# A two-layer cross-attention kernel on one core: the transposed softmax goes from SBUF to SBUF, and three steps named `acc` stand elsewhere in the order

## The chip, the core and the metric

The kernel runs on one NeuronCore of a Trainium2 chip. Its engines are TensorE (PE in the profile; its weight loads are PEld), VectorE (DVE), ScalarE (ACT), GpSimd (POOL) and SyncE (SP), each with an instruction stream of its own that is worked off in order and waits on semaphores. Matmuls write PSUM, and the other engines move data between PSUM and SBUF. DMA transfers are issued from an engine's queue, here SP's and ACT's. The metric is the device time of the whole program in microseconds. The median before is 1039.65 us of 3 runs, 1038.39 to 1040.42.

## The reference

For each of 8 batches, with x1 = x[b] and x2 = ctx[b], both 512 channels by 1024 positions:

```
q = Wq x1 + bq ; k = Wk x2 + bk ; v = Wv x2 + bv        (64, 64 and 512 rows)
x = v softmax(q^T k)^T + x1                             (softmax over k's positions)

theta = th_w x + th_b ; phi = phi_w x2 + phi_b ; g = g_w x2 + g_b   (256 rows each)
y = (theta^T phi / 1024) g^T  ->  w_w y + w_b, batch norm with stored statistics, + x
```

The second layer has no softmax. The kernel therefore multiplies phi and g first: phi g^T is taken from the 512 x 512 matrix x2 x2^T (the "gram") and from the row sums of x2.

## The kernel before

Matmuls keep the precision of fp32 by splitting each operand into a high part (a copy rounded to fp32r) and a low part (the rest), and by multiplying three pairs of parts. So almost each operand costs ScalarE a copy and VectorE or GpSimd a subtraction.

The order of the work is written out by hand. `FIRST` (batch 0) and `LATER` (batches 1 to 7) hold, for each of `pe`, `act`, `dve` and `pool`, a string of steps such as `S:3` or `v:0`, and `order()` turns it into the sequence that the engine runs. A plus sign marks work for the next batch. The steps that matter here:

- `S:t` (t = 0 to 7): scores of 128 queries against all keys. TensorE multiplies, VectorE takes the maximum, ScalarE the exponential, VectorE scales (`n:t`) and transposes 32 x 32 blocks (`tr:t`) into the tiles `tp0`, `tp1`, two t to a tile.
- `move(b, p)` on SP turns pair p of them into the full transpose: it writes both tiles to a DRAM tensor `turn` (2 transfers of 512 KB) and reads it back into `mv1` or `mv2` in another order (8 transfers of 128 KB).
- `T:t`: ScalarE (`do_T`, line 832) and VectorE (line 996) split `mv` into the operand `pt` of the product with v, which TensorE runs as `PV`. PV of half 0 waits for the low part of T:3, PV of half 1 for that of T:7.
- `x2T:m`: the split of the transposed context for the gram (`L`, `G` on TensorE).
- `k`, `q`, then `k2`, `q2`: sums and splits of k and q. S:0 waits for `klo` and `qlo`, the results of `k2` and `q2` on VectorE.
- `v:m`: v for 128 positions. The PSUM bank of TensorE's `v:2` in the later batches is the one that VectorE's `v:0` frees, that of `Y:0` in batch 0 the one that VectorE's `v:6` frees.
- `acc`: a bias row of 256 numbers from phi_w and the row sums of x2. In batch 0 GpSimd computes it in 17 instructions after a scaling of `br` (lines 1084 to 1095) and in the later batches VectorE does in 8 (line 913). ScalarE's `acc` (line 796) takes the high part and waits for the eighth sum; `accl` (line 918 on VectorE) or the end of GpSimd's `acc` gives the low part, and TensorE's `psi` (line 631) multiplies it.
- `s8` on GpSimd: four columns that VectorE's first `Y` needs.

Of the kernel before, what the change touches and what calls it, by code (L numbers as in the profile page):

```python
# [4 lines left out]
F = mybir.dt.float32  # L5
# [18 lines left out]
    k=2, q=2, S=8, GT=2, M=2, B=2, g=40, psi=1,  # L24
# [31 lines left out]
def use_g(b, r):  # L56
# [28 lines left out]
    pool=(  # L85
        "x2T:0 x2T:1 x2T:2 x2T:3 x2T:4 x2T:5 x2T:6 x2T:7 s8 acc Y:0 Y:1 Y:2 Y:3 PV:0,0 PV:0,1 PV:0,2 PV:0,3 PV:1,0 "
        "PV:1,1 PV:1,2 PV:1,3"
# [10 lines left out]
    act=(  # L98
# [6 lines left out]
    dve=(  # L105
# [26 lines left out]
def xattn_kernel(nc, x, ctx2, ctx2T, wkT, wqT, wvT, wpgT, thT, woT, brow, cols, out):  # L132
    with ExitStack() as stack:
        def sem(name):
            return stack.enter_context(nc.semaphore(name))
# [3 lines left out]
        def at(name, shape, dt, offset):  # L139
            return nc.alloc_sbuf_tensor_at(name, shape, dt, offset=offset)  # L140
# [69 lines left out]
        qlo = at("qlo", [128, 1024], R, o)  # L210
        mv2 = at("mv2", [128, 4, 2, 256], F, o); o += 4096
        P = at("P", [128, 1024], F, o)
# [13 lines left out]
        bm = at("bm", [128, 2, 2, 512], R, o)  # L226
        mv1 = at("mv1", [128, 4, 2, 256], F, o)
        x2T_f0 = at("x2T_f0", [128, 4, 512], F, o); o += 8192
# [6 lines left out]

        turn = nc.dram_tensor("turn", [4, 128, 4, 2, 256], F).ap()
        s_turn = [sem(f"s_turn{t}") for t in range(8)]
        sems = {n: sem("s_" + n) for n in PER}
# [54 lines left out]
        def mv(p):  # L293

            return mv2 if p == 3 else mv1
# [24 lines left out]
        def moved(i):  # L320

            j = i % 2 * 2
            return [mv(i // 2)[:, j:j + 2, t, :].rearrange("p j (u n) -> p u j n", u=8) for t in range(2)]

# [50 lines left out]
        def _(eng):  # L375
# [24 lines left out]
            def move(b, p):  # L400


                for t in range(2):
                    wait(eng, "tr", b, 2 * p + t)
                    eng.dma_start(turn[p, :, :, t, :], tp[p % 2][:, t, :].rearrange("p (i n) -> p i n", i=4))\
                        .then_inc(s_turn[2 * p + t], 16)
                for t in range(2):
                    eng.wait_ge(s_turn[2 * p + t], 16 * (b + 1))
                for k in range(2):
                    if p == 0:  # L410
                        wait(eng, "x2Tlo", b, 7)
                    elif p == 3:
                        wait(eng, "S", b, 7)
                    else:
                        wait(eng, "Tlo", b, 2 * p - 2 + k)
                    for i in range(4):
                        eng.dma_start(mv(p)[32 * i:32 * i + 32, 2 * k:2 * k + 2, :, :],
                                      turn[p, 64 * k:64 * k + 64, i, :, :].rearrange("(j a) t n -> a j t n", a=32))\
                            .then_inc(s_mv[2 * p + k], 16)

# [285 lines left out]
        def _(eng):  # L706
# [118 lines left out]
            def do_T(b, t):  # L825
                eng.wait_ge(s_mv[t], 64 * (b + 1))
                if t == 0:
                    wait(eng, "g", b, use_g(b, 3))
                if t == 4:
                    wait(eng, "M", b, 1)  # L830
                for k in range(2):
                    last = act(pt_half(t, HI)[k], moved(t)[k], ACT.Copy)  # L832
                done(last, "Thi")
# [36 lines left out]
        def _(eng):  # L870
# [87 lines left out]
            def do_tr(b, t):  # L958
                wait(eng, "norm", b, t)
                if t == 2:  # L960
                    wait(eng, "x2Tlo", b, 3 if b else 7)
                if t >= 4:
                    for i in range(2):
                        eng.wait_ge(s_mv[t // 2 * 2 - 4 + i], 64 * (b + 1))
                done(eng.transpose(tp[t // 2 % 2][:, t % 2, :], P[:, :]), "tr")  # L965
# [19 lines left out]
            def do_Y(b, c):  # L985
                wait(eng, "g", b, G_Y + c)
                if c == 0:
                    eng.wait_ge(s_br8, 1)
                    wait(eng, "s8", b)
                done(stt(out=yf[:, c, :], in0=br[:, :], scalar=scol8[:, c:c + 1], in1=bank_of(G_Y + c)[:, 0:256],  # L990
                         op0=ALU.mult, op1=ALU.add), "gf")
# [171 lines left out]
```

## Time and profile before

| | us |
|---|---|
| median of 3 runs | 1039.65 |
| the profiled execution | 1039.65 |
| its span | 1037.8 |
| TensorE busy | 1028.6 (99%) |
| VectorE busy | 685.1 (66%) |
| ScalarE busy | 494.9 (48%) |
| GpSimd busy | 296.4 (29%) |

The granted TensorE clock is 1.00 over the span. The chain that ended last is TensorE for 89%, VectorE for 4%, GpSimd and DMA for 2% each. The costliest group is the product with v (line 661): 353.8 us in 1536 matmuls. The DMA queues moved 155.46 MB, and the write to `turn` and the reads from it land 3.2 and 2.9 us after their issue (medians). A row of the timeline gives the start of a run of like instructions, how long it took, their count, and in brackets how long the engine had stood idle before it and who released it. Times are counted from the start of the span.

### The profile page before, as it was taken

The numbers are of one execution on the slowest core, as the hardware profiler recorded it, in microseconds if no ns is written. First come the engines' busy times: TensorE is split into PE (matmuls) and PEld (weight loads), VectorE is DVE, ScalarE is ACT, GpSimd is POOL, SyncE is SP. The second block draws the span as 40 slices with busy tenths as digits, with TensorE's granted clock in tenths as the row PEclk, the third lists the DMA queues.
The fourth block names the chain that finished last, engine by engine and source line by source line (L and its number), as shares of the span: only waits on it lengthen the run. The fifth ranks groups of instructions, "written<-read, shape, count | busy, mean of one in ns | idle before, by whom it ended". The sixth has DMA issues, their size and how long they took to land.

```text
span 1037.8 us, 13692 instructions
## 1 busy us (share of the span) xinstructions
PE 1028.6 (99%) x5055; PEld 850.6 (82%) x5055; DVE 685.1 (66%) x970; ACT 494.9 (48%) x835; POOL 296.4 (29%) x253
## 2 busy tenths in 40 slices
PE   9999999999999999999999999999999999999998
PEld 7778888888888887888888888888887888878887
DVE  6994497834888258882588825887268862688625
ACT  7653564425554264542744427454275532655321
POOL 1652370122701236012360123502144022540220
PEclk9999999999999999999999999999999999999999
DMA  7747153561545514455244552455434464335602
GB/s 255 217 142 234 65 200 123 163 222 54 170 129 189 190 63 161 139 186 183 72 153 152 178 178 87 137 163 181 165 103 136 150 201 142 122 123 163 193 31 81
DMA packets 94226, 155.46 MB, mean 150 GB/s; under 512 B 10064, under 2 KB 43728, under 8 KB 94160
## 3 DMA queue, kind: packets, MB, share of 16 engines
q1 hardware_dynamic: 84944, 137.80, 40.6%
q10 hardware_dynamic: 9216, 16.78, 4.8%
q8 instruction: 41, 0.67, 0.3%
q14 instruction: 25, 0.20, 0.1%
HBM read 104.22 MB, written 50.33 MB: 149 GB/s over the span
## 4 chain that ended last, share of the span: by engine, by line
PE 89%; DVE 4%; POOL 2%; DMA 2%; ACT 1%; issue 1%; SPq 0%; ACTq 0%; DVEq 0%
PE pG L661 33%; PE pG L567 14%; PE pG L672 8%; PE pG L575 6%; PE pG L606 4%; PE pG L582 4%; PE pT L694 3%; PE pG L694 3%; PE pS L618 2%; PE pM L649 2%; PE pT L514 2%; PE pT L618 2%; PE pM L640 2%; PE pS L503 2%; POOL x1s L1067 1%; DMA x2T_f<-in_ctx2T_dram 1%
## 5 line engine op out<-in xcount | busy, mean ns | idle before, releaser
L661 PE MATMUL pG<-pt,vT 128*128 128x512 f32 x1536 | 353.8, 389 | 0.0
L661 PEld LDWEIGHTS pG<-pt,vT 128*128 128x128 f32 x1536 | 286.9, 188 | 58.6
L1103 POOL TENSOR_TENSOR xms<-xr,xms 128x512 fp32r<-128x512 f32 x64 | 87.4, 1372 | 327.6 <-ACT xms L854 327.6
L567 PE MATMUL pG<-wv,x2s 128*128 128x512 f32 x720 | 169.3, 392 | 0.3
L567 PEld LDWEIGHTS pG<-wv,x2s 128*128 128x128 f32 x720 | 133.9, 188 | 31.7 <-issue 2.5
L1019 DVE SCALAR_TENSOR_TENSOR xr<-pG,cl,xr 128x512 f32<-128x512 f32 x64 | 47.9, 749 | 167.8 <-PE pG L661 167.8
L854 ACT ACTIVATE xms<-xr 128x512 fp32r<-128x512 f32 x64 | 40.4, 631 | 174.9 <-DVE xr L1019 174.9
L996 DVE TENSOR_TENSOR pt<-mv,pt 128x512 fp32r<-128x512 f32 x128 | 83.3, 693 | 56.3 <-ACT pt L832 56.1
L1099 POOL TENSOR_TENSOR ys<-yf,ys 128x256 fp32r<-128x256 f32 x32 | 29.6, 926 | 284.0 <-ACT ys L823 284.0
L832 ACT ACTIVATE pt<-mv 128x512 fp32r<-128x512 f32 x128 | 73.3, 622 | 57.9 <-DMA mv<-turn 42.0
L1074 POOL TENSOR_TENSOR x2Ts<-x2T_f,x2Ts 128x512 fp32r<-128x512 f32 x64 | 86.2, 1374 | 37.3 <-ACT x2Ts L792 37.3
L672 PE MATMUL pG<-xms,wth 128*128 128x512 f32 x384 | 88.3, 389 | 0.0
L672 PEld LDWEIGHTS pG<-xms,wth 128*128 128x128 f32 x384 | 72.1, 188 | 15.0
L1067 POOL TENSOR_TENSOR x1s<-st,x1s 128x512 fp32r<-128x512 f32 x56 | 71.2, 1307 | 45.8 <-ACT x1s L744 45.8
L965 DVE STREAM_TRANSPOSE tp<-P 128x1024 f32<-128x1024 f32 x64 | 79.5, 1241 | 1.3
L779 ACT ACTIVATE vT<-pG 128x512 fp32r<-128x512 f32 x62 | 36.9, 598 | 73.4 <-PE pG L567 73.4
L575 PE MATMUL pG<-x2Ts 128*128 128x512 f32 x256 | 63.0, 397 | 0.2 <-POOL x2Ts L1074 0.2
L575 PEld LDWEIGHTS pG<-x2Ts 128*128 128x128 f32 x256 | 46.8, 188 | 15.5 <-issue 5.8
L792 ACT ACTIVATE x2Ts<-x2T_f 128x512 fp32r<-128x512 f32 x64 | 37.2, 623 | 42.4 <-DMA x2T_f<-in_ctx2T_dram 42.4
L785 ACT ACTIVATE P<-pT,nmax 128x1024 f32<-128x1024 f32 x32 | 35.7, 1115 | 38.9 <-DVE tp L965 36.6
L606 PEld LDWEIGHTS pG<-wpg,gram 128*128 128x128 f32 x384 | 47.5, 191 | 5.4 <-issue 4.8
L606 PE MATMUL pG<-wpg,gram 128*128 128x256 f32 x384 | 49.6, 285 | 1.7 <-DVE vT L946 1.7
(145 smaller groups left out, 1486.6 us busy)
## 6 DMA issues: line engine op xcount, KB each, us to landing
turn<-tp SPq DMA_DIRECT2D x64, 512.0 KB, 3.2
mv<-turn SPq DMA_DIRECT2D x256, 128.0 KB, 2.9
x2T_f<-in_ctx2T_dram SPq DMA_DIRECT2D x32, 512.0 KB, 4.8
xr<-in_x_dram ACTq DMA_DIRECT2D x64, 256.0 KB, 5.2
st<-in_ctx_dram SPq DMA_DIRECT2D x31, 512.0 KB, 6.4
st<-in_x_dram SPq DMA_DIRECT2D x29, 512.0 KB, 4.2
out_dram<-oh SPq DMA_DIRECT2D x32, 256.0 KB, 2.0
out_dram<-xr SPq DMA_DIRECT2D x31, 256.0 KB, 8.0
```

The costliest lines, as they stand in the source:

```text
L567: last = mm(bank, x2s[:, l, c, 128 * m:128 * m + 128], wv[:, r, c, :], start=(c == 0 and n == 0), stop=(c == 3 and n == 2))
L575: last = mm(bank, x2Ts[:, HI, m, 128 * r:128 * r + 128], x2Ts[:, LO, m, :], start=(m == 0), stop=(m == 7))
L606: last = mm(bank[:, 0:256], gram[:, l, d, 128 * c:128 * c + 128], wpg[:, r, d, 0:256], start=(d == 0 and n == 0), stop=(d == 3 and n == 2))
L661: last = mm(bank, vT[:, l, m, 128 * c:128 * c + 128], pt(h)[:, r, m, :], start=(m == 0 and n == 0), stop=(m == 7 and n == 2))
L672: last = mm(bank, wth[:, l, c, 128 * k:128 * k + 128], xms(h)[:, c, r, :], start=(c == 0 and n == 0), stop=(c == 3 and n == 2))
L694: last = mm(bank, bm[:, l, k, 128 * c:128 * c + 128], th[:, r, k, 512 * h:512 * h + 512], start=(k == 0 and n == 0), stop=(k == 1 and n == 2))
L832: last = act(pt_half(t, HI)[k], moved(t)[k], ACT.Copy)
L965: done(eng.transpose(tp[t // 2 % 2][:, t % 2, :], P[:, :]), "tr")
L996: last = tt(pt_half(t, LO)[k], moved(t)[k], pt_half(t, HI)[k].bitcast(F), ALU.subtract)
L1067: done(tt(x1s(b)[:, LO, c, cols], st1(b, c)[:, cols], x1s(b)[:, HI, c, cols].bitcast(F), ALU.subtract), "x1lo")
L1074: done(tt(x2Ts[:, LO, m, :], x2T_raw(b, m), x2Ts[:, HI, m, :].bitcast(F), ALU.subtract), "x2Tlo")
L1103: done(tt(xms(h)[:, c, LO, :], xr[c][:, :], xms(h)[:, c, HI, :].bitcast(F), ALU.subtract), "xlo")
```

## The change

Three things are changed.

1. `move` no longer goes through DRAM. For each pair it waits for the second transpose and then issues 16 transfers of 64 KB straight from `tp` to `mv`, four for each block j of 32 source partitions, all on SP's queue. The first eight count for T:2p, the last eight for T:2p+1. The tiles `mv1` and `mv2` hold the two t outermost, and the two places that read or await them are adapted.
2. ScalarE's `acc` stands earlier: in batch 0 right behind `GT:1`, ahead of `w:7` and `v:6` (it was behind `T:3`), in the later batches right behind `k`, ahead of `x2T:1` (it was behind `x2T:4`). VectorE's `accl` in the later batches stands ahead of `q` (it was behind it).
3. On GpSimd in batch 0, `acc` stands ahead of `s8`, and VectorE's first `Y` no longer waits for the scaled `br`, since `s8` now comes after it.

```diff
@@ -69,7 +69,7 @@
-        "S:3 T:0 G:1 G:2 T:1 G:3 GT:0 S:4 GT:1 w:7 v:6 v:7 T:2 S:5 T:3 acc Y:0 Y:1 Y:2 S:6 Y:3 psi S:7 w:8 xr:0 "
+        "S:3 T:0 G:1 G:2 T:1 G:3 GT:0 S:4 GT:1 acc w:7 v:6 v:7 T:2 S:5 T:3 Y:0 Y:1 Y:2 S:6 Y:3 psi S:7 w:8 xr:0 "
...
@@ -208,7 +208,7 @@
-        mv2 = at("mv2", [128, 4, 2, 256], F, o); o += 4096
+        mv2 = at("mv2", [128, 2, 4, 256], F, o); o += 4096
...
-        mv1 = at("mv1", [128, 4, 2, 256], F, o)
+        mv1 = at("mv1", [128, 2, 4, 256], F, o)
...
@@ -233,8 +233,6 @@
-        turn = nc.dram_tensor("turn", [4, 128, 4, 2, 256], F).ap()
-        s_turn = [sem(f"s_turn{t}") for t in range(8)]
...
@@ -320,7 +318,7 @@
-            return [mv(i // 2)[:, j:j + 2, t, :].rearrange("p j (u n) -> p u j n", u=8) for t in range(2)]
+            return [mv(i // 2)[:, t, j:j + 2, :].rearrange("p j (u n) -> p u j n", u=8) for t in range(2)]
...
@@ -400,23 +398,18 @@
             def move(b, p):
-                for t in range(2):
-                    wait(eng, "tr", b, 2 * p + t)
-                    eng.dma_start(turn[p, :, :, t, :], tp[p % 2][:, t, :].rearrange("p (i n) -> p i n", i=4))\
-                        .then_inc(s_turn[2 * p + t], 16)
-                for t in range(2):
-                    eng.wait_ge(s_turn[2 * p + t], 16 * (b + 1))
-                for k in range(2):
+                wait(eng, "tr", b, 2 * p + 1)
+                for j in range(4):
                     if p == 0:
                         wait(eng, "x2Tlo", b, 7)
                     elif p == 3:
                         wait(eng, "S", b, 7)
                     else:
-                        wait(eng, "Tlo", b, 2 * p - 2 + k)
+                        wait(eng, "Tlo", b, 2 * p - 2 + j // 2)
                     for i in range(4):
-                        eng.dma_start(mv(p)[32 * i:32 * i + 32, 2 * k:2 * k + 2, :, :],
-                                      turn[p, 64 * k:64 * k + 64, i, :, :].rearrange("(j a) t n -> a j t n", a=32))\
-                            .then_inc(s_mv[2 * p + k], 16)
+                        eng.dma_start(mv(p)[32 * i:32 * i + 32, :, j, :],
+                                      tp[p % 2][32 * j:32 * j + 32, :, 256 * i:256 * i + 256])\
+                            .then_inc(s_mv[2 * p + j // 2], 16)
...
@@ -823,7 +816,7 @@
-                eng.wait_ge(s_mv[t], 64 * (b + 1))
+                eng.wait_ge(s_mv[t], 128 * (b + 1))
...
@@ -985,7 +978,6 @@
                 if c == 0:
-                    eng.wait_ge(s_br8, 1)
                     wait(eng, "s8", b)
```

In the strings that aren't shown, GpSimd's `... x2T:7 s8 acc Y:0` has become `... x2T:7 acc s8 Y:0` in `FIRST`, ScalarE's `k x2T:1 x2T:2 x2T:3 x2T:4 acc x2T:5 q` has become `k acc x2T:1 x2T:2 x2T:3 x2T:4 x2T:5 q` in `LATER`, and VectorE's `acc k q accl v:0` has become `acc k accl q v:0`. The wait in `do_tr` counts to 128 like that in `do_T`.

ScalarE in batch 0, from the split of the gram's last block on. `accs_first` is the step `acc`, `wth` is `w:7`, `vT` is `v:6` and `v:7`, `pt` is `T:2`. Before:

```order
L819 ACTIVATE gram<-pM 128x2x128
L721 ACTIVATE wth<-wth_f 128x1024
L779 ACTIVATE vT<-pG 128x512 x2
L832 ACTIVATE pt_85<-mv_128 128x8x64 x2
L785 ACTIVATE P,rsum<-pT,nmax 128x1024
L832 ACTIVATE pt_85<-mv_128 128x8x64 x2
L796 ACTIVATE accs_first<-acc_first 128x256
L823 ACTIVATE ys<-yf 128x256 x3
```

Now:

```order
L812 ACTIVATE gram<-pM 128x2x128
L789 ACTIVATE accs_first<-acc_first 128x256
L714 ACTIVATE wth<-wth_f 128x1024
L772 ACTIVATE vT<-pG 128x512 x2
L825 ACTIVATE pt_85<-mv_128 128x8x64 x2
L778 ACTIVATE P,rsum<-pT,nmax 128x1024
L825 ACTIVATE pt_85<-mv_128 128x8x64 x2
L816 ACTIVATE ys<-yf 128x256 x3
```

`accs_first` has gone up past one split of weights, two of v, two of the turned softmax and an exponential.

ScalarE in batch 1, from the first piece of the transposed context on (`x2Ts`); `accs` is `acc`, and `qhi` is `q2`. Before:

```order
L792 ACTIVATE x2Ts<-x2T_f_126 128x512
L751 ACTIVATE k_101<-pS 64x1024
L792 ACTIVATE x2Ts<-x2T_f_126 128x512 x3
L792 ACTIVATE x2Ts<-x2T_f_129 128x512
L796 ACTIVATE accs<-acc 128x256
L792 ACTIVATE x2Ts<-x2T_f_129 128x512
L758 ACTIVATE q_105<-pT 64x1024
L779 ACTIVATE vT<-pG 128x512
L792 ACTIVATE x2Ts<-x2T_f_129 128x512 x2
L772 ACTIVATE qhi<-pT 128x1024
```

Now:

```order
L785 ACTIVATE x2Ts<-x2T_f_126 128x512
L744 ACTIVATE k_101<-pS 64x1024
L789 ACTIVATE accs<-acc 128x256
L785 ACTIVATE x2Ts<-x2T_f_126 128x512 x3
L785 ACTIVATE x2Ts<-x2T_f_129 128x512 x2
L751 ACTIVATE q_105<-pT 64x1024
L772 ACTIVATE vT<-pG 128x512
L785 ACTIVATE x2Ts<-x2T_f_129 128x512 x2
L765 ACTIVATE qhi<-pT 128x1024
```

`accs` has gone up past four pieces of the transposed context, which now stand between it and `q`.

VectorE in batch 1: the eight sums of `acc`, then `k` (`pM`), `q` (`pT`) and `accl` (`accs`). Before:

```order
L913 SCALAR_TENSOR_TENSOR acc<-wpg,scol,br 128x256
L913 SCALAR_TENSOR_TENSOR acc<-wpg,scol,acc 128x256 x7
L927 SCALAR_TENSOR_TENSOR pM<-pS,cl,k_101 64x256 x4
L933 SCALAR_TENSOR_TENSOR pT<-pT,cl,q_105 64x1024 x2
L918 TENSOR_TENSOR accs<-acc,accs 128x256
L946 TENSOR_TENSOR vT<-pG,vT 128x512
L942 TENSOR_TENSOR qlo<-pT,qhi 128x1024
L946 TENSOR_TENSOR vT<-pG,vT 128x512
L938 TENSOR_TENSOR klo<-pM,khi 128x512
```

Now:

```order
L906 SCALAR_TENSOR_TENSOR acc<-wpg,scol,br 128x256
L906 SCALAR_TENSOR_TENSOR acc<-wpg,scol,acc 128x256 x7
L920 SCALAR_TENSOR_TENSOR pM<-pS,cl,k_101 64x256 x4
L911 TENSOR_TENSOR accs<-acc,accs 128x256
L926 SCALAR_TENSOR_TENSOR pT<-pT,cl,q_105 64x1024 x2
L939 TENSOR_TENSOR vT<-pG,vT 128x512
L935 TENSOR_TENSOR qlo<-pT,qhi 128x1024
L939 TENSOR_TENSOR vT<-pG,vT 128x512
L931 TENSOR_TENSOR klo<-pM,khi 128x512
```

`accs` has changed places with the two instructions of `q`.

## Rows read from the trace of the kernel before

**Rows 1.** the page, part 1: TensorE's busy time
```profile
PE 1028.6 (99%) x5055; PEld 850.6 (82%) x5055; DVE 685.1 (66%) x970; ACT 494.9 (48%) x835; POOL 296.4 (29%) x253
```

**Rows 2.** who TensorE waited for: us in total, times, longest
```profile
PE pM L631 <- DVE accs L918: 0.8, 1, 0.8
```

**Rows 3.** timeline of TensorE, batch 0: start us, us, instruction, idle before
```profile
60.95 1.31 PE L606 MATMUL pG<-wpg,gram 128*128 128x256 f32 x9 [1.66 <-DVE vT L946]
```

**Rows 4.** timeline of ScalarE, batch 0
```profile
57.82 1.06 ACT L721 ACTIVATE wth<-wth_f 128x1024 fp32r<-128x1024 f32 x1
58.85 1.08 ACT L779 ACTIVATE vT<-pG 128x512 fp32r<-128x512 f32 x2
...
65.88 0.40 ACT L796 ACTIVATE accs_first<-acc_first 128x256 fp32r<-128x256 f32 x1
```

**Rows 5.** timeline of GpSimd, batch 0
```profile
62.63 0.74 POOL L1093 TENSOR_TENSOR acc_first<-accp,acc_first 128x256 f32<-128x256 f32 x1
```

**Rows 6.** timeline of VectorE, batch 0
```profile
60.17 0.68 DVE L946 TENSOR_TENSOR vT<-pG,vT 128x512 fp32r<-128x512 f32 x1
```

**Rows 7.** timeline of ScalarE, batch 4
```profile
529.44 2.18 ACT L792 ACTIVATE x2Ts<-x2T_f 128x512 fp32r<-128x512 f32 x4
531.74 0.42 ACT L796 ACTIVATE accs<-acc 128x256 fp32r<-128x256 f32 x1
532.07 0.62 ACT L792 ACTIVATE x2Ts<-x2T_f 128x512 fp32r<-128x512 f32 x1
532.59 1.01 ACT L758 ACTIVATE q<-pT 64x1024 f32<-64x1024 f32 x1
```

**Rows 8.** timeline of VectorE, batch 4
```profile
526.07 5.64 DVE L913 SCALAR_TENSOR_TENSOR acc<-wpg,scol,acc 128x256 f32<-128x256 f32 x7
...
533.63 2.61 DVE L933 SCALAR_TENSOR_TENSOR pT<-pT,cl,q 64x1024 f32<-64x1024 f32 x2 [0.21 <-ACT q L758]
536.16 0.93 DVE L918 TENSOR_TENSOR accs<-acc,accs 128x256 fp32r<-128x256 f32 x1
537.02 0.67 DVE L946 TENSOR_TENSOR vT<-pG,vT 128x512 fp32r<-128x512 f32 x1
...
539.35 0.67 DVE L938 TENSOR_TENSOR klo<-pM,khi 128x512 fp32r<-128x512 f32 x1
```

**Rows 9.** timeline of TensorE, batch 4
```profile
537.38 0.40 PE L631 MATMUL pM<-accs,ones_r 128*128 128x256 f32 x2
537.74 3.01 PE L567 MATMUL pG<-wv,x2s 128*128 128x512 f32 x12
540.69 0.50 PE L618 MATMUL pS<-khi,qhi 64*128 64x512 f32 x2
```

**Rows 10.** chain that ended last, in order of time: start us, us, what
```profile
374.34 10.89 PE pG L672 x48
...
503.09 10.88 PE pG L672 x48
...
630.60 10.88 PE pG L672 x48
```

**Rows 11.** transfers of line 417: issue ns min/median/max, then landing us
```profile
L417 SPq DMA_DIRECT2D mv<-turn x256: 302/427/1880, 45.6 to 981.0; - x128
...
DMA to landing us min/median/max: 2.4/2.9/5.0
```

**Rows 12.** SyncE's waits: us in total, times, longest
```profile
SPq L260 <- DMA turn<-tp: 98.3, 32, 4.7
```

**Rows 13.** timeline of VectorE, batch 4, later
```profile
578.97 1.29 DVE L996 TENSOR_TENSOR pt<-mv,pt 128x512 fp32r<-128x512 f32 x2
```

**Rows 14.** timeline of TensorE, batch 4, later
```profile
581.25 2.00 PE L661 MATMUL pG<-pt,vT 128*128 128x512 f32 x8
```

**Rows 15.** timeline of TensorE at the launch
```profile
1.44 4.21 PE L701 MATMUL pT<-warm 128*128 128x512 f32 x9 [1.44 <-DVE warm L1056]
...
8.64 0.61 PE L531 MATMUL pG<-wv,x2s 128*128 128x512 f32 x2
```

More of the change, by code:

```diff
@@ L85 @@
     pool=(
-        "x2T:0 x2T:1 x2T:2 x2T:3 x2T:4 x2T:5 x2T:6 x2T:7 s8 acc Y:0 Y:1 Y:2 Y:3 PV:0,0 PV:0,1 PV:0,2 PV:0,3 PV:1,0 "
+        "x2T:0 x2T:1 x2T:2 x2T:3 x2T:4 x2T:5 x2T:6 x2T:7 acc s8 Y:0 Y:1 Y:2 Y:3 PV:0,0 PV:0,1 PV:0,2 PV:0,3 PV:1,0 "
         "PV:1,1 PV:1,2 PV:1,3"
@@ L963, in do_tr @@
                     for i in range(2):
-                        eng.wait_ge(s_mv[t // 2 * 2 - 4 + i], 64 * (b + 1))
+                        eng.wait_ge(s_mv[t // 2 * 2 - 4 + i], 128 * (b + 1))
                 done(eng.transpose(tp[t // 2 % 2][:, t % 2, :], P[:, :]), "tr")
```

4 rows, old and new, of tables (act, dve) are left out of this document.

## The prediction

> **What bounds the kernel now.** I read the busy times first. TensorE is busy for 1028.6 us, 99% of the span [rows 1], so a faster transfer or a shorter chain elsewhere can give back only what TensorE idles, and whatever makes TensorE wait is added in full. The waits of TensorE come next: the longest is 1.66 us, once, for VectorE's low part of v [rows 3], and 0.8 us once for the low part of the bias row (`accs`) [rows 2]. The chain in order of time shows the period: the products with theta's weights start at 374.34, 503.09 and 630.60 us, so one period is 128.75 and the next 127.51 us [rows 10]. The longer one holds the 0.8 us wait and is 1.24 us over; six of the seven batches behind batch 0 show the short period to within 0.25 us. All that the change could win is these 1.24 us, about 0.25 us in batch 1, and part of the 1.66. So the question is whether one of the moved steps now stands in an engine's way. A moved step that waits blocks everything queued behind it, and for that I read ScalarE's, VectorE's and GpSimd's timelines around each new place.
>
> **Part 1: `acc` on ScalarE in batch 0.** It waits for GpSimd's eighth sum, which starts at 62.63 and takes 0.74, so it is there at 63.37 us [rows 5]. In its new place ScalarE reaches it at 57.82, where the split `w:7` starts now [rows 4]. ScalarE then stands still for 5.6 us, and `w:7`, `v:6`, `v:7` and T:2 are queued behind. After the wait the step takes 0.33 us to the next start (like 531.74 to 532.07 in [rows 7]; it is the 0.40 us row in batch 0), `w:7` 1.03 us (57.82 to 58.85), and the first of two copies of v half of 1.08 us [rows 4]: 63.42 + 0.33 + 1.03 + 0.54 = 65.3 us, and with a tenth for the semaphore 65.4 us. VectorE's low part of `v:6` starts at 60.17 us now [rows 6], not held by ScalarE. It becomes 5.2 us later, and TensorE's `Y:0`, which waits for it and starts at 60.95 us [rows 3], goes to 66.15. VectorE works the following steps (a transpose, `v:7`, a maximum, `Y:0`) back to back in its order, so they move by the same 5.2 us and nothing catches up. GpSimd's sums start as before, since what they wait for has not moved. They could end a little earlier while VectorE idles, or ScalarE could be slower: bounds 4.7 and 5.5, value **+5.2 us**.
>
> The Trainium skill speaks to the lower bound: "GPSIMD Engine Reference", section "Specifications", says that GpSimd's SBUF interfaces are shared with VectorE and that VectorE instructions with two SBUF inputs contend with it. By that rule the last sums would gain from VectorE's idle time; by the row, 0.74 us for the last one, there is little left to gain.
>
> **Part 2: TensorE's clock in that gap.** TensorE now idles 1.66 us before `Y:0` [rows 3]; it will idle 6.9. Full speed follows the 1.66 us. The only longer rest in the trace is the launch: there nine matmuls of 512 columns start within 4.0 us (1.44 to 5.44, 444 ns each), about the 1.2 GHz level, and from 8.64 us on two such take 0.61 us in all, where 1.1 would be due at the launch's rate, so that is the 2.4 GHz level [rows 15]. The granted clock is given as 1.0 throughout, so I read the level from the spacing. If the 6.9 us act like the launch, the next 6.7 us (the launch's lasted from 1.44 to somewhat before 8.64) run at half rate. `Y`'s matmuls of 256 columns start 0.13 us apart (nine in 1.31 us, [rows 3]) and would take 0.22, so 30 of them cost 6.7 instead of 3.9 us, 2.7 us lost in round numbers, less some 0.2 that TensorE would wait for VectorE anyway. Bounds 0 (as after 1.66 us) and 2.5; since 6.9 is four times the longest rest after which full speed is seen, I take a drop, and **+2.0 us** for it.
>
> The Trainium skill, "TensorE: Matmul & The Clock Gate", section "What's actually happening", says that an idle engine falls back to the 1.2 GHz level and rises only after sustained activity. By that the gap does cost clock. No row before the change shows such a fall inside the run.
>
> **Part 3: `acc` on ScalarE in batches 1 to 7.** It waits for VectorE's eighth sum, the end of a run that starts at 526.07 and takes 5.64 [rows 8], and starts at 531.74 us both now and then. Four pieces of the transposed context fill that time now, 529.44 to 531.62 [rows 7]. With `acc` ahead of them ScalarE waits 2.3 us behind `k`, and the pieces come after: next start 532.07, then five pieces of 0.52 us (532.07 to 532.59) give 534.67 for `q`, against 532.59 now [rows 7]: 2.08 us later. VectorE's `q` waits for it already [rows 8] and goes from 533.63 to 535.71. `accl` is no longer behind it, which wins 0.86 us (536.16 to 537.02). So `v:0` starts at 537.02 + 2.08 - 0.86 = 538.24. TensorE's `v:2` needs the bank that `v:0` frees: 0.72 us later as now (537.02 to 537.74, [rows 8, 9]), 538.96, so **1.22 us** late. S:0 then follows 2.95 us behind (537.74 to 540.69, [rows 9]); `klo`, now at 539.35 with 1.3 us to spare, comes some 1.8 us later at about 541.8 and just makes it. Nothing takes this back: VectorE's sums of the next batch start behind TensorE's last product. In the long period this delay replaces the one it has, so 0 there; six batches pay: 6 x 1.22 = **+7.3 us**. Bounds 6 x 1.0 and 6 x 1.4.
>
> **Part 4: the direct move.** Per pair, behind its second transpose, now: 98.3/32 = 3.1 us of wait for the write [rows 12], 8 issues of 0.427 us, 2.9 us to landing [rows 11], 9.4 us for the last piece and 7.7 for the first half. Then: 16 issues, 6.8 us, plus 2.9, is 9.7 us, and 6.3 for the first half. The trace has no transfer of this kind; the landings of the 128 KB pieces are 2.4 to 5.0 us, and I take the median, since those are small pieces into the same tiles. TensorE has no wait for `pt` in any batch, so either sign is hidden: **0**. Its cover in the tightest place is 1.0 us (VectorE's two subtractions for T:3 end at 580.2, and the first product with v starts at 581.25, [rows 13, 14]). SP's loads of the next batch and its stores are behind the move and have all of the product with v as cover. `s8` behind `acc` on GpSimd is needed by VectorE's `Y:0`, behind TensorE's at 66.15 us in the new schedule; behind the sums (63.37) come ScalarE's copy of 0.40 us [rows 4], one more subtraction of about 0.74 and `s8` itself, so it is there by 65 us: 0. The removed wait is implied by it: 0. The new tile layout changes strides and no instruction: 0.
>
> **Sum.** The profiled execution took 1039.65 us, which is the median too (span 1037.8 and 1.85 around it). 1039.65 + 5.2 + 2.0 + 7.3 = 1054.15, predicted **1054 us**.
>
> **Rivals.**
> - *The clock stays up.* For it: full speed behind 1.66 us of rest. Against: 6.9 us is far longer. 1039.65 + 5.2 + 7.3 = 1052.2 us. Here the skill's clock rule stands against it.
> - *Only one of the two stalls reaches TensorE*, because the chain behind it has slack that I don't see in the rows, for instance if VectorE's `v:0` does not wait behind `q`. 1039.65 + 7.2 or + 7.3: 1047 us. Against: both chains are followed step by step to TensorE with no free time between.
> - *The transfers come late.* If landings of SBUF to SBUF are all like the longest of now, 5.0 us, T:3's operand comes 0.3 + 2.1 = 2.4 us later, 1.4 beyond the cover, in each of 8 batches: 1054 + 11 = 1065 us. Half of it gives 1059. Against: half the bytes pass and none goes to DRAM.
> - *Faster.* The bias sums are done before ScalarE comes to the wait, and the earlier `accl` removes TensorE's wait for `accs`: 1039.65 - 1.24 - 0.25 = 1038.2 us. It decides if VectorE's eighth sum ended by 529.44 us, the end of `k`; it ends 2.3 us later [rows 7, 8], and GpSimd's 5.6 us later than needed. So this needs sums that take 60% of their time.
>
> **How the numbers follow.** Forecast 0.50 (1052.8 to 1055.8 its own range), clock stays 0.20, one stall alone 0.12, late transfers 0.08, faster 0.05, and 0.05 for effects that cancel to no change. A measurement of this kernel tells about 0.2% from no change, 2.1 us. Slower is 0.50 + 0.20 + 0.12 + 0.08 = 0.90, same 0.05, faster 0.05. The range reaches down over the one-stall case to 1046.5 and up to 1057.5 for part of the late transfers and the bounds of the sums; left out are faster, same and most of the late transfers, under 0.2.
>
> **What would show it.** In the profile after: ScalarE idle for over 5 us ahead of `accs_first`, TensorE idle for 6 to 7 us ahead of its first `Y`, and matmul spacing behind it near double (part 2), or not. In each later batch ScalarE idle for 2.3 us behind `k`, `q` about 2.1 us later, TensorE idle for 1.3 us between `psi` and `v:2`, and periods of 128.7 us all alike. No wait of TensorE for `pt`. I am wrong if periods stay at 127.5, if TensorE's gap in batch 0 stays below 3 us, or if TensorE waits for the products' operand.

## The result and the profile after

The changed kernel takes 1046.67 us (median of 4 runs, 1046.25 to 1047.21); the kernel before takes 1039.29 (4 runs, 1038.39 to 1040.42). The ratio is 1.007, 95% interval 1.0053 to 1.0088: slower, as forecast, by about half of the forecast's 14.5 us. 1046.67 lies at the low end of the range given (1046.5 to 1057.5). The profiled execution took 1045.72 us, its span is 1043.8, so 6.0 us of the two spans are to be explained. The medians lie 7.4 us apart: this profiled execution is 0.5 us below the fastest timed one of its kernel, and the one profiled before (1039.65) lies above the median of its kernel. In the experiments below, one execution of e6 (4481 us) and one of the kernel before (2072 us) lie far off all others and are left out of the ratios. Lines of this kernel are 7 lower than before up to the wait that `do_Y` has lost, and 8 lower behind it.

The page after, part 1, beside [rows 1]: TensorE's busy time grows by only 0.5 us, VectorE's shrinks by 6.4.

```profile
PE 1029.1 (99%) x5055; PEld 852.4 (82%) x5055; DVE 678.7 (65%) x970; ACT 495.2 (47%) x835; POOL 293.4 (28%) x253
```

The chain in order of time, the product with theta's weights (start us, us, what), beside [rows 10]:

```profile
125.39 10.88 PE pG L665 x48
...
253.38 10.88 PE pG L665 x48
...
380.99 10.88 PE pG L665 x48
508.58 10.88 PE pG L665 x48
636.25 10.88 PE pG L665 x48
```

These starts give periods of 127.6 and 127.7 us, and 128.0 for the first, where 128.7 was forecast. In TensorE's timeline this product first starts at 118.90 before and 125.23 after. So batch 0 costs 6.33 us, and the seven periods behind it together take 893.73 us against 894.10, a gain of 0.37: 6.33 - 0.37 = 5.96, which is the 6.0 of the spans.

The 0.37 us can't be put down to the change. TensorE's wait for `accs`, which makes one period of the kernel before longer, comes and goes between executions: in the traces of e1, e2 and e11, which keep the old order in the later batches, it stands in another batch (seven periods of 894.56, 894.00 and 893.87 us), and in those of e4 and e13 in none (892.79 and 892.69). The four traces with the new order (this one, e3, e7 and e9) don't have it and take 893.73 to 894.10. So in the later batches the change costs 0.9 to 1.4 us against an execution without that wait, and about nothing against one with it.

**Batch 0 after.** ScalarE, beside [rows 4]:

```profile
63.42 0.42 ACT L789 ACTIVATE accs_first<-acc_first 128x256 fp32r<-128x256 f32 x1 [5.26 <-POOL acc_first L1085]
63.74 1.04 ACT L714 ACTIVATE wth<-wth_f 128x1024 fp32r<-128x1024 f32 x1
64.69 1.06 ACT L772 ACTIVATE vT<-pG 128x512 fp32r<-128x512 f32 x2
```

GpSimd, beside [rows 5], and VectorE, beside [rows 6]:

```profile
62.66 0.72 POOL L1085 TENSOR_TENSOR acc_first<-accp,acc_first 128x256 f32<-128x256 f32 x1
```

```profile
65.30 0.69 DVE L939 TENSOR_TENSOR vT<-pG,vT 128x512 fp32r<-128x512 f32 x1 [5.00 <-ACT vT L772]
```

TensorE, beside [rows 3]:

```profile
66.09 6.68 PE L599 MATMUL pG<-wpg,gram 128*128 128x256 f32 x36 [6.79 <-DVE vT L939]
72.71 0.50 PE L611 MATMUL pS<-khi,qhi 64*128 64x512 f32 x2
```

The stall goes from GpSimd's sum over ScalarE and VectorE to TensorE, which starts at 66.09 instead of 60.95 and then needs 6.68 us for 36 products. In stretches of the run (window us, its length, busy us of PE, PEld, DVE, ACT and POOL with counts, granted clock, DMA share, GB/s):

```profile
62.00:64.00 2.00, 0.00 (x0) 0.00 (x0) 0.00 (x0) 0.58 (x2) 1.39 (x3) 1.00 0.41 99
64.00:66.00 2.00, 0.00 (x0) 0.00 (x0) 0.70 (x2) 2.00 (x4) 0.86 (x2) 0.54 0.41 98
66.00:68.00 2.00, 1.91 (x9) 1.94 (x10) 2.00 (x3) 0.79 (x2) 0.00 (x0) 0.50 0.00 0
68.00:70.00 2.00, 2.00 (x11) 2.00 (x11) 1.82 (x3) 1.11 (x3) 0.00 (x0) 0.50 0.00 0
70.00:71.00 1.00, 1.00 (x7) 1.00 (x6) 0.96 (x4) 1.00 (x3) 0.00 (x0) 0.52 0.00 0
71.00:72.00 1.00, 1.00 (x10) 1.00 (x10) 0.97 (x2) 0.43 (x2) 0.48 (x1) 1.00 0.00 0
```

While TensorE idles the granted clock goes from 1.00 (the 2.4 GHz level) to 0.50 (1.2 GHz), and it is back at 1.00 some 5 us after the matmuls have begun: 9 to 11 of them in 2 us, then 10 in 1 us.

**Batch 4 after**, VectorE, beside [rows 8]; the times are later by 5.5 us throughout, so lengths and distances are to be compared:

```profile
531.56 4.58 DVE L906 SCALAR_TENSOR_TENSOR acc<-wpg,scol,acc 128x256 f32<-128x256 f32 x7
...
537.75 1.07 DVE L911 TENSOR_TENSOR accs<-acc,accs 128x256 fp32r<-128x256 f32 x1
540.14 2.61 DVE L926 SCALAR_TENSOR_TENSOR pT<-pT,cl,q 64x1024 f32<-64x1024 f32 x2 [1.32 <-ACT q L751]
542.66 0.67 DVE L939 TENSOR_TENSOR vT<-pG,vT 128x512 fp32r<-128x512 f32 x1
```

ScalarE, beside [rows 7]:

```profile
536.17 0.42 ACT L789 ACTIVATE accs<-acc 128x256 fp32r<-128x256 f32 x1 [1.14 <-DVE acc L906]
536.49 2.70 ACT L785 ACTIVATE x2Ts<-x2T_f 128x512 fp32r<-128x512 f32 x5
539.10 1.01 ACT L751 ACTIVATE q<-pT 64x1024 f32<-64x1024 f32 x1
```

TensorE, beside [rows 9]:

```profile
542.87 0.40 PE L624 MATMUL pM<-accs,ones_r 128*128 128x256 f32 x2
543.39 3.01 PE L560 MATMUL pG<-wv,x2s 128*128 128x512 f32 x12
546.34 0.50 PE L611 MATMUL pS<-khi,qhi 64*128 64x512 f32 x2
```

The seven sums take 4.58 us where they took 5.64, ScalarE waits 1.14 us where 2.3 were forecast, and TensorE goes from `psi` to S:0 in 3.47 us instead of 3.31. GpSimd shows why. Before:

```profile
526.40 1.31 POOL L1074 TENSOR_TENSOR x2Ts<-x2T_f,x2Ts 128x512 fp32r<-128x512 f32 x1 [1.70 <-ACT x2Ts L792]
530.13 9.36 POOL L1074 TENSOR_TENSOR x2Ts<-x2T_f,x2Ts 128x512 fp32r<-128x512 f32 x7 [2.43 <-ACT x2Ts L792]
```

After:

```profile
531.96 1.29 POOL L1066 TENSOR_TENSOR x2Ts<-x2T_f,x2Ts 128x512 fp32r<-128x512 f32 x1 [1.78 <-ACT x2Ts L785]
537.18 4.04 POOL L1066 TENSOR_TENSOR x2Ts<-x2T_f,x2Ts 128x512 fp32r<-128x512 f32 x3 [3.93 <-ACT x2Ts L785]
```

GpSimd's subtractions for the transposed context follow ScalarE's copies. Before, 1.31 us of them and the 1.58 us from 530.13 to 531.71 run beside VectorE's sums (2.9 us in all); after, with the copies held back behind `acc`, only 1.29 us do.

Single sums show what that does. A sum that GpSimd doesn't disturb takes 0.48 us. This one of the kernel before begins while GpSimd's first subtraction runs, and ends 0.28 us behind it (527.99 against 527.71). One of k's sums, which reads one of its two inputs from PSUM (`pS`), begins while another subtraction runs and keeps its length:

```profile
526.59 1.40 DVE L913 SCALAR_TENSOR_TENSOR acc<-wpg,scol,acc 128x256 f32<-128x256 f32 x1
...
531.39 1.48 POOL L1074 TENSOR_TENSOR x2Ts<-x2T_f,x2Ts 128x512 fp32r<-128x512 f32 x1
532.03 0.47 DVE L927 SCALAR_TENSOR_TENSOR pM<-pS,cl,k 64x256 f32<-64x256 f32 x1
```

Two of the seven sums are held in this way in each later batch before (1.40 to 1.60 us each), and one after (1.40 to 1.45 us).

**The transfers after**, beside [rows 11]: issue ns min/median/max and landing us min/median/max.

```profile
L410 SPq DMA_DIRECT2D mv<-tp x512: 585/596/1854, 42.5 to 988.9; - x171
...
DMA to landing us min/median/max: 2.0/2.0/5.6
```

An issue takes 0.596 us, not 0.427, and lands in 2.0 us, not 2.9. The bytes moved fall from 155.46 to 121.94 MB. TensorE doesn't wait for `pt` in this kernel.

### The profile page after: what moved, and what is told of

Same layout as the page of the kernel before. It is cut to its first block, busy times and chain, and to the rows that moved or that the text cites. A ratio compares the mean times of both kernels' runs of the same rounds, so it can differ in the third digit from the quotient of the medians.

```text
span 1043.8 us, 13884 instructions
## 1 busy us (share of the span) xinstructions
PE 1029.1 (99%) x5055; PEld 852.4 (82%) x5055; DVE 678.7 (65%) x970; ACT 495.2 (47%) x835; POOL 293.4 (28%) x253
## 2 busy tenths in 40 slices
DMA packets 80916, 121.94 MB, mean 117 GB/s; under 512 B 13136, under 2 KB 46800, under 8 KB 80848
## 4 chain that ended last, share of the span: by engine, by line
PE 86%; DVE 7%; ACT 3%; POOL 2%; issue 1%; DMA 0%; SPq 0%; ACTq 0%; DVEq 0%; POOLq 0%
PE pG L654 33%; PE pG L560 11%; PE pG L665 8%; PE pG L568 5%; PE pG L599 5%; PE pT L687 4%; PE pG L687 4%; PE pG L575 4%; DVE acc L906 3%; PE pS L611 2%; PE pM L633 2%; PE pM L642 2%; DVE pT L926 2%; PE pT L611 2%; ACT x2Ts L785 1%
## 5 line engine op out<-in xcount | busy, mean ns | idle before, releaser
L1066 POOL TENSOR_TENSOR x2Ts<-x2T_f,x2Ts 128x512 fp32r<-128x512 f32 x64 | 83.7, 1335 | 49.0 <-ACT x2Ts L785 49.0
L599 PEld LDWEIGHTS pG<-wpg,gram 128*128 128x128 f32 x384 | 49.6, 199 | 10.2 <-issue 9.7
```

What stands on the lines that cost most here:

```text
L599: last = mm(bank[:, 0:256], gram[:, l, d, 128 * c:128 * c + 128], wpg[:, r, d, 0:256], start=(d == 0 and n == 0), stop=(d == 3 and n == 2))
L1066: done(tt(x2Ts[:, LO, m, :], x2T_raw(b, m), x2Ts[:, HI, m, :].bitcast(F), ALU.subtract), "x2Tlo")
```

## The experiments

Each is told against the kernel before, run in turn on the same chip (medians 1038.6, 1039.2 and 1039.4 us in the three sets of runs). In a diff `-` is the kernel named first.

**e1: the direct move alone.** All parts of the change in `mv1`, `mv2`, `moved`, `move` and the counts of the waits; no step `acc` or `s8` moves.

> The kernel before with the direct move alone; all orders as before. My theory: TensorE never waits for the turned softmax, so the time is that of before, 1039.3 us, within 1 us either way, and the period stays near 127.5 us with one of 128.7. VectorE's eight sums (acc) in the later batches keep their 5.6 us for seven. Rival (DMA traffic): it was the traffic through DRAM that slowed VectorE's sums, so here they take about 4.6 us for seven, and the wait for accs in batch 3 goes: 1038 us.

1041.1 us (11 runs), ratio 1.0021 (1.0012 to 1.003): not free, against my theory. The sums take their 5.6 us as before, so the rival falls too. TensorE waits for the following (us in total, times, longest):

```profile
PE pM L624 <- POOL accs_first L1088: 1.2, 1, 1.2
...
PE pG L654 <- DVE pt L989: 0.8, 1, 0.8
```

Both stand in batch 0, and ScalarE's copies of the moved blocks show their origin:

```profile
54.65 1.15 ACT L825 ACTIVATE pt<-mv 128x512 fp32r<-128x512 f32 x2 [2.12 <-DMA mv<-tp]
...
60.67 1.16 ACT L825 ACTIVATE pt<-mv 128x512 fp32r<-128x512 f32 x2 [0.90 <-DMA mv<-tp]
...
65.79 1.16 ACT L825 ACTIVATE pt<-mv 128x512 fp32r<-128x512 f32 x2 [1.20 <-DMA mv<-tp]
```

The third starts at 64.84 before. It delays ScalarE's `acc` (65.88, [rows 4], to 66.85 us), and TensorE's `psi` waits for that. From `Y:0` to theta's product it is 59.72 us (60.60 to 120.32), before 57.95 (60.95 to 118.90): 1.77 us lost. Two of the seven periods behind it take 127.8 us instead of 127.5.

**e11: the same move in half as many transfers.** The kernel of e1, with

```
-  for i in range(4):
-      eng.dma_start(mv(p)[32 * i:32 * i + 32, :, j, :], tp[p % 2][32 * j:32 * j + 32, :, 256 * i:256 * i + 256])
+  for i in range(2):
+      eng.dma_start(mv(p)[64 * i:64 * i + 64, :, j, :], tp[p % 2][64 * (j % 2):64 * (j % 2) + 64, :, 256 * i:256 * i + 256])
```

> The kernel before with the direct move alone, as in the first of these runs, but each pair goes in 8 transfers of 128 KB instead of 16 of 64 KB; the same bytes move, and every block of the softmax's rows lands in another place than the reference wants. Theory A, the number of issues: each issue holds SyncE's queue for 0.60 us, so 8 of them take 4.8 us per pair instead of 9.5, the waits of the copies of pt in batch 0 (2.1, 0.9 and 1.2 us in the first run) go, the first product with theta's weights starts at 118.9 us +-0.4 as in the kernel before, and the time is 1039.0 +-0.8. Rival B, the transfer between two places of SBUF is itself slow (or an issue costs by its bytes, so 1.2 us each): the waits and the 1.4 us of batch 0 stay, time 1040.5 to 1041.5.

1039.78 us (11 runs), ratio 1.0004 (0.9995 to 1.0013). The issues:

```profile
L410 SPq DMA_DIRECT2D mv<-tp x256: 590/608/2036, 43.7 to 978.3; - x128
```

An issue costs 0.608 us with twice the bytes, so between 64 and 128 KB the price goes by the transfer and not by the byte. (The kernel leaves out the order in which the blocks have to land, so its result isn't the reference's; bytes and waits are those of the direct move.) The three copies of `pt` have no wait on the transfers, and from `Y:0` to theta's product it is 57.95 us again (62.23 to 120.18). Theory A holds; rival B falls. The absolute start that I had given for that product (118.9) is missed by 1.3 us, because this execution was already 1.3 us late before its first such transfer (the first product with `wq` on `x1s_first` starts at 24.95 us, before at 23.68), which the change can't reach.

**e2: ScalarE's `acc` in batch 0 alone.** In `FIRST`, `act`:

```
-  GT:1 w:7 v:6 v:7 T:2 S:5 T:3 acc Y:0
+  GT:1 acc w:7 v:6 v:7 T:2 S:5 T:3 Y:0
```

> The kernel before with ScalarE's acc of batch 0 ahead of w:7 and nothing else. My theory: this one word makes the whole loss: TensorE idles about 6.8 us ahead of its first Y (5.1 more than before), the granted clock falls to 0.50 behind it, and the time is 1045.5 to 1047 us. Rival (the loss is spread over the parts): the time rises by 4 us or less.

1045.58 us (5 runs), ratio 1.0065 (1.0052 to 1.0077). One line of the order makes nearly all of the loss. TensorE:

```profile
65.58 6.59 PE L606 MATMUL pG<-wpg,gram 128*128 128x256 f32 x36 [6.78 <-DVE vT L946]
```

with a granted clock of 0.50 from 64 to 70 us.

**e4: GpSimd's `acc` ahead of `s8` in batch 0 alone.** In `FIRST`, `pool`: `s8 acc` becomes `acc s8`.

> The kernel before with GpSimd's acc ahead of s8 in batch 0 and nothing else. I had costed this at nothing, with ScalarE's earlier acc as its cover. Without the cover: s8 waits for the low part, which waits for ScalarE's acc behind T:3 (65.9 us); s8 is there at 67.4 us and VectorE's first Y moves from 63.6 to 67.4, so TensorE waits about 3.5 us ahead of Y:2: 1043 us, or 1044 to 1045 if the clock falls in that gap. Rival (GpSimd's order has slack): 1039.3 us.

1043.6 us (4 runs), ratio 1.0047 (1.0033 to 1.0061). Alone, this edit costs what the prediction had at nothing: GpSimd's `acc` waits for ScalarE's, which is still at its old place, and `s8` with VectorE's `Y:0` waits behind it (67.49 us instead of 63.63). TensorE:

```profile
60.90 4.60 PE L606 MATMUL pG<-wpg,gram 128*128 128x256 f32 x24 [1.67 <-DVE vT L946]
68.07 2.61 PE L606 MATMUL pG<-wpg,gram 128*128 128x256 f32 x12 [2.58 <-issue]
```

In the change it is hidden, since ScalarE's `acc` is early there: `s8` ends at 64.95 us. It also shows the clock fall behind a rest of 1.67 us (24 products take 4.60 us; granted 0.50 from 62 to 65 us, and again from 69 to 71 us, behind the 2.58), where the same rest of 1.66 us before [rows 3] was followed by the full rate.

**e9: the change without its edits to batch 0's order.** `FIRST` as before, all else as after.

> The changed kernel with batch 0 in the order of before (ScalarE's acc behind T:3, GpSimd's s8 ahead of acc, the wait for the scaled br back). My theory: all of the loss was in batch 0, so 1038.8 us, within 0.6 of before. Rival (the later batches cost too): 1041 us or more.

1041.23 us (9 runs), ratio 1.0023 (1.0013 to 1.0033). 5.4 of the 7.4 us of the change are gone with one table. The rest is that of e1: TensorE waits 1.09 us for `accs_first` and 0.9 for `pt` in batch 0. I had expected 1038.8, still holding the move to be free. The rival has the time, but not the place: the seven later periods take 893.89 us, no more than before.

**e7: TensorE kept busy in the gap.** The changed kernel, and ahead of `Y:0` in batch 0 24 products whose result nobody reads:

```
+  if b == 0 and c == 0:
+      wait(eng, "exp", 0, 4)
+      for _ in range(24):
+          mm(pS[:, 0, :], wv[:, 0, 0, 0:128], wv[:, 0, 0, :], start=True, stop=True)
```

> The changed kernel with 24 matmuls of 512 columns that nothing reads, on TensorE between S:5 and Y:0 of batch 0, into a score bank that is free then. They fill 5.4 of the 6.8 us. Theory (the rest costs clock): the granted clock stays at 1.0, the first 36 matmuls of Y take 4.9 us instead of 6.7, and the time is 1.2 to 1.8 us under the changed kernel, 1045 us. Rival (the slow stretch has another cause, such as the order of the other engines): no gain, 1046.7 us.

```profile
59.09 5.73 PE L596 MATMUL pS<-wv 128*128 128x512 f32 x24
66.17 4.91 PE L603 MATMUL pG<-wpg,gram 128*128 128x256 f32 x36 [1.35 <-issue]
71.01 0.50 PE L615 MATMUL pS<-khi,qhi 64*128 64x512 f32 x2
```

The clock stays at 1.00, the 36 products take 4.91 us, and S:6 starts 1.70 us earlier than after (72.71): that is the clock's part, measured. But the time is 1048.42 us (4 runs), ratio 1.009 (1.0077 to 1.0104), beside 1046.67 and 1.007 (1.0053 to 1.0088) for the change. My expectation of 1045 is missed; the two intervals overlap, so it is not shown that the filler makes the kernel slower. In the trace the first product with theta's weights starts 3.1 us later than after (128.33 against 125.23), because TensorE comes to the second half of the product with v sooner than its operands do:

```profile
104.88 7.30 PE L658 MATMUL pG<-pt,vT 128*128 128x512 f32 x24 [2.39 <-DVE pt L992]
```

ScalarE's copy for T:7 waits 4.85 us for its transfer there; SyncE issues this batch's 64 transfers until 99.7 us. The clock falls again behind it (0.52 in 106 to 108 us). So the issues of part 4 have no cover left in batch 0 once the gap is filled.

**e3: `acc` and `accl` in batches 1 to 7 alone.** In `LATER`: ScalarE `k acc x2T:1`, VectorE `k accl q`, as in the change; the move through DRAM stays.

> The kernel before with the two words moved in the later batches (ScalarE's acc right behind k, VectorE's accl ahead of q), softmax still turned through DRAM. My theory now: ScalarE's copies and so GpSimd's subtractions no longer run beside VectorE's sums, which take 4.6 us for seven instead of 5.6; v:2 of TensorE starts only 0.1 to 0.2 us later than before, the periods are 127.6 us and all alike, and the time is 1039 us, within 0.6. Rival (DMA traffic of the turn made the sums slow): the sums take 5.6 us, v:2 is 1.2 us late in each batch, and the time is 1046 us, as I had predicted for this part.

1040.24 us (11 runs), ratio 1.0012 (1.0003 to 1.002). VectorE:

```profile
526.09 4.53 DVE L913 SCALAR_TENSOR_TENSOR acc<-wpg,scol,acc 128x256 f32<-128x256 f32 x7
```

The sums are short with the transfers of before, so it isn't the DMA's lighter load that shortens them. The periods are 127.6 to 127.7 us but for batch 1's 128.2. The time is above the 1039 +-0.6 that I expected, and far below the rival's 1046.

**e6: GpSimd held back, nothing else.** The kernel before, with every step `acc` at its old place; in GpSimd's `x2T`:

```
+  if b and m:
+      wait(eng, "acc", b, 7)
```

> The kernel before with one more wait: in batches 1 to 7 GpSimd's subtractions of the transposed context from the second on wait for VectorE's eighth sum. ScalarE's copies and the DMA traffic stay beside the sums. Theory A (GpSimd slows the sums): seven sums take 4.6 us instead of 5.6, ScalarE's acc and q come up to 1 us earlier, the wait for accs in batch 3 is gone, and the time is 1038 us. Theories B (ScalarE's copies) and C (DMA traffic): the sums stay at 5.6 us and the time at 1039.3 us or above it.

VectorE, then GpSimd:

```profile
524.95 4.52 DVE L913 SCALAR_TENSOR_TENSOR acc<-wpg,scol,acc 128x256 f32<-128x256 f32 x7
```

```profile
529.64 9.24 POOL L1076 TENSOR_TENSOR x2Ts<-x2T_f,x2Ts 128x512 fp32r<-128x512 f32 x7 [3.06 <-DVE acc L913]
```

Some of ScalarE's copies run beside the sums here as before (from 528.33 us on), so it isn't ScalarE either: it is GpSimd. One sum in each batch is still held, by the first subtraction, which has no wait. Periods are 127.28 to 127.30 us but for batch 1's 128.32, and the time is 1037.34 us (11 runs), ratio 0.9982 (0.9973 to 0.9991): less than both kernels, for one wait.

**e5: GpSimd beside all of the sums.** The changed kernel, with GpSimd's first subtraction of batches 1 to 7 made four times, one after the other (same result). 

> The changed kernel with GpSimd's first subtraction of the transposed context made four times over in batches 1 to 7 (same operands and result), so that GpSimd works beside VectorE's sums again while ScalarE stands still. Theory A (GpSimd beside VectorE slows the sums): seven sums take 5.3 us or more instead of 4.6, v:2 is late by about 1 us in each batch, and the time is 1046.7 + 7 x 0.7 to 1.0 = 1051.5 to 1053.7 us. Theory B (ScalarE's copies beside them slow the sums) and theory C (DMA traffic): the sums stay at 4.6 us and the time at 1046.7 us.

VectorE, then GpSimd:

```profile
411.80 7.32 DVE L907 SCALAR_TENSOR_TENSOR acc<-wpg,scol,acc 128x256 f32<-128x256 f32 x7
```

```profile
412.22 4.15 POOL L1069 TENSOR_TENSOR x2Ts<-x2T_f,x2Ts 128x512 fp32r<-128x512 f32 x3 [1.77 <-ACT x2Ts L786]
416.44 1.36 POOL L1073 TENSOR_TENSOR x2Ts<-x2T_f,x2Ts 128x512 fp32r<-128x512 f32 x1
```

1071.96 us (4 runs), ratio 1.0326 (1.0306 to 1.0346): right in kind, and far above what I expected. The sums grow by 2.74 us (four of the seven are held in each batch, each to 0.28 us behind the end of a subtraction) and the shorter periods by 2.7 (127.6 to 130.3). Three of the seven periods are 132, because the granted clock falls behind TensorE's waits of 3.29, 2.86 and 2.80 us; behind the other four, of 2.79 to 2.81 us, it stays at 1.00. I had reckoned with a longer wait only, on fewer slowed sums and at full clock.

**e13: another order in batch 0.** The kernel before; ScalarE's `w:7` behind T:2, VectorE's low part of `v:6` ahead of `n:4`.

> The kernel before with the order of batch 0 alone changed: ScalarE splits w:7 behind T:2, VectorE takes the low part of v:6 ahead of n:4. Theory: TensorE's 1.66 us wait ahead of its first product of Y is VectorE's low part of v:6, so it shrinks to under 0.7 and the time falls by 1.0 +-0.4 against the kernel before. Rival: the next wait takes its place, time within 0.3 us of the kernel before.

1039.44 us (11 runs), ratio 1.0003 (0.9994 to 1.0012). The 1.66 us wait splits into two of 1.02 and 1.04, the second ahead of the 13th product of `Y`. My theory is missed and the rival holds.

**e12: both together.** e6's wait, e13's order, and `accl` ahead of `q`.

> The kernel before with three changes of order: GpSimd's second to eighth subtraction for the transposed context waits for VectorE's eighth sum (batches 1 to 7); VectorE's low part of the bias row ahead of q's (batches 1 to 7); in batch 0 ScalarE splits w:7 behind T:2 and VectorE takes the low part of v:6 ahead of n:4. The move through DRAM stays. Theory: the shorter periods of 127.29 us of the run with GpSimd's wait stay, and in batch 0 the 1.66 us wait ahead of Y:0 shrinks to under 0.7: 1037.3 - 1.1 = 1036.2 +-0.6. Rival: the wait ahead of Y:0 is only put off to T:2 or w:7 behind it (TensorE waits for the split weight), and the time is 1037.3 +-0.4; no gain over the run with GpSimd's wait.

1037.18 us (11 runs), ratio 0.9982 (0.9973 to 0.9991): no gain over e6 that could be told, as the rival had it. e6 and e12 lie 1.9 and 2.2 us below the kernel before in their own sets, and over 9 us below the changed one.

## Why the prediction was right in sign and twice too large

The profiled execution was forecast at 1054.15 us and took 1045.72, 8.4 less. By its parts:

- **Part 1, right.** +5.2 forecast, +5.14 measured (66.09 against 60.95). Each step of the path came within 0.1 us, and e2 shows it alone.
- **Part 2, right in kind.** +2.0 forecast. The 36 products take 6.68 instead of 4.91 us, 1.77; e7 gives 1.70. Of the 6.92 us that the two make behind S:6, 0.46 are taken back ahead of `mts`, where TensorE waited 0.30 us before and doesn't now, and 0.13 in the product with `mts`, which takes 2.88 us instead of 3.01. Parts 1 and 2: 7.2 forecast, 6.33 measured. The launch's row was a fair model of the fall; the stay at the low level was 5 us where I had read up to 6.7 off it. The Trainium skill's rule on the idle clock ("TensorE: Matmul & The Clock Gate", section "What's actually happening") is borne out by the 0.50 rows for this gap; shorter rests went either way (e4, e5).
- **Part 3, the step that failed.** The term was six batches x 1.22 = +7.3; the seven periods together gave -0.37. The failed sentence is that ScalarE's `acc`, which waits for VectorE's eighth sum, "starts at 531.74 us both now and then". It took the length of the sums, 5.64 us, as fixed. They are long because GpSimd works beside them, and the same edit that makes ScalarE wait holds GpSimd's subtractions back: 4.58 us, 1.06 less. Put into the forecast's own chain, 1.22 - 1.06 = 0.16 per batch, and TensorE's way from `psi` to S:0 did grow by 3.47 - 3.31 = 0.16. Against it stands the wait for `accs` that one period before has (128.75 us) and none after; as said above, executions of the old order have it or not, so the two nearly cancel in these two traces by chance. The prediction's own sign of being wrong, periods that stay near 127.5 us, came in. The rest of that chain held: five copies behind `acc`, `q` late, `accl` won.
- **Part 4, wrong but covered.** Issues were costed at 0.427 us from transfers of another kind, and take 0.596: 16 of them 9.5 us per pair, not 6.8. Landing was 0.9 us shorter. Alone this costs 1.77 us in batch 0 (e1), where the pairs follow closer; I had looked for the tightest place in batch 4 only. In the change TensorE's gap of 6.79 us hides it, and in the later batches TensorE doesn't wait for it. `s8`'s zero is right in the change and wrong alone (e4).

The rival "only one of the two stalls reaches TensorE" gave 1047 us and has the time nearly to the point, by another mechanism than its own: the chain had no slack, its first link got shorter. That the time is met so closely is luck. The rival "faster" came nearer in kind, as it asked for shorter sums; it needed 60% of their time, and they took 81%. The forecast looked at the wrong side of the matter too: I had weighed what the sums in batch 0 gain when VectorE idles (0.74 to 0.72 us, nothing), and not what VectorE's sums gain when GpSimd does.

How far the mechanism goes can be counted in the traces. In all thirteen, a sum of `acc` in the later batches that begins while one of GpSimd's subtractions of 128x512 runs is held until 0.28 us behind its end, 115 of 115 times; it takes 1.39 to 1.51 us instead of 0.48 (up to 1.60 where the two begin together). With none held the seven would take 3.6 us (7 x 0.52 from start to start). One held gives 4.52 to 4.68 us (after, e3, e6), two 5.46 to 5.64 (before) and four 7.25 to 7.33 (e5). So the price goes by the number of GpSimd's instructions that meet such a sum, 0.9 to 1.1 us each. The Trainium skill says in "GPSIMD Engine Reference", section "Specifications", that VectorE's instructions with two SBUF inputs contend with GpSimd's; the sums have two such inputs (`wpg` and `acc`), and e3, e5 and e6 agree with it, as do k's sums with one input in PSUM, which take 0.47 to 0.49 us beside GpSimd too. That the interface itself is the cause, and not something else that comes with GpSimd's work, no run here shows.

Left open: of e1's loss by the median (2.5 us) its trace has 1.77 us in batch 0 and 0.46 in the later periods; the start of a run varies by over 1 us (23.3 to 25.0 us for the first product with `wq`), so I don't read the rest. e3's median is 1.6 us over before while its span is only 0.5 over; the profiled execution before has the wait for `accs`, and against the two without it (e4, e13) the seven periods of e3 are 1.3 to 1.4 us longer, which would account for most of it. Why the clock fell behind a rest of 1.67 us in e4 and not behind 1.66 us before, and behind three of seven rests of about 2.8 us and more in e5, no run shows: the length of the rest alone doesn't tell it.

## What to carry to other kernels

A duration in a profile belongs to what ran beside it: before a term is built on the length of a run of instructions, look at what the neighbouring engines do in that stretch, and whether the edit moves that. A wait put on an engine off the critical path can pay, as e6 shows, if it keeps that engine from slowing the one that others wait for. An order with an early wait is costed by the queue behind it in the fullest stage (here batch 0), and a new kind of transfer by its issues on the queue, in that same stage.

## What the runs showed of the hardware

- A VectorE sum of 128x256 with two inputs in SBUF that begins while GpSimd subtracts 128x512 ends 0.28 us behind GpSimd's instruction: 1.4 to 1.6 us instead of 0.48. VectorE's instructions with one of two inputs in PSUM keep their length (k's sums, 0.47 to 0.49 us).
- It can go the other way. VectorE's subtraction `accs` takes 1.07 us in the change, where GpSimd's row from 537.18 us runs beside it. In e6 it takes 0.41 us though GpSimd works beside it too, and there GpSimd's instruction is the longer one, 1.72 us instead of 1.29:

```profile
534.66 1.72 POOL L1076 TENSOR_TENSOR x2Ts<-x2T_f,x2Ts 128x512 fp32r<-128x512 f32 x1
...
534.81 0.41 DVE L918 TENSOR_TENSOR accs<-acc,accs 128x256 fp32r<-128x256 f32 x1
```

- An SBUF-to-SBUF issue costs SyncE's queue 0.60 us at 64 KB and 0.61 at 128 KB; the pieces from DRAM cost 0.43 us at 128 KB. They land in 2.0 and 2.4 us, those from DRAM in 2.9 (medians).
- TensorE's granted clock fell to 0.50 in the rest of 6.8 us and came back some 5 us after work began. Behind 1.66 to 1.81 us of rest it stayed at 1.00 in six traces (before, e1, e3, e6, e9, e11) and fell in one (e4, 1.67 us); behind 2.39 (e7), 2.58 (e4), 2.80, 2.86 and 3.29 us (e5) it fell, and behind four more rests of 2.79 to 2.81 us in e5 it stayed.
